# Graph attention turned round to 128 keys by 512 queries, with the expert stage split off

## The reference

```python
lK, lV = ln(x) @ Wlk, ln(x) @ Wlv + blv            # keys, values
local = where(adj, (masked_x @ Wlq) @ lK.T / 16, -1e9)
top = max(local.max(1), global_score, es)
le, ge, ee = exp(local - top), exp(global_score - top), exp(es - top)
denom = le.sum(1) + ge + ee
res = le/denom @ lV + ge/denom * gV + ee/denom * eV
x1 = x + maximum(res, masked_x)
xf = ln(x1); n = ln(xf) * ln_g + ln_b
xa = n @ attn_w.T + attn_b + xf
h = gelu(xa[expert] @ fc1[e].T + b1[e]); y = h @ fc2[e].T + b2[e]
out = x1 + gelu(y @ next_w.T + next_b)
```

## Time and profile before

| | us |
|---|---|
| median of 3 runs | 1241.9 (1238.49 to 1241.97) |
| span of the profiled execution | 1237.6 |
| PE / PE weight load busy | 1173.4 / 1003.3 |
| DVE / ACT / POOL busy | 782.8 / 550.7 / 458.5 |
| instructions | 21869 |

### The profile page before, as it was taken

The page is one execution under the profiler, slowest core; times in us unless marked ns, Lnnn a source line. Parts: engine busy times, 40 slices in busy tenths (PEclk is TensorE's granted clock), DMA queues, the critical chain, the costliest instruction groups (busy, mean ns, idle before and its releaser), DMA issues.

```text
span 1237.6 us, 21869 instructions
## 1 busy us (share of the span) xinstructions
PE 1173.4 (95%) x6524; PEld 1003.3 (81%) x6524; DVE 782.8 (63%) x1750; ACT 550.7 (44%) x981; POOL 458.5 (37%) x512
## 2 busy tenths in 40 slices
PE   4679999999999999999999999999988999999997
PEld 3557888888888888888888888888877887888886
DVE  6985555655556555565555555555577777877773
ACT  4534433344333443333433334433445565565654
POOL 4552223222232222322222322223237466655661
PEclk9799999999999999999999999999999999999999
DMA  7551111101111111111111111111346354454511
GB/s 231 176 148 33 56 34 34 47 34 55 34 34 46 34 55 34 34 42 38 48 42 34 42 38 43 46 34 42 99 163 195 99 177 151 163 195 131 174 69 51
DMA packets 70476, 100.15 MB, mean 81 GB/s; under 512 B 5936, under 2 KB 45872, under 8 KB 70448
## 3 DMA queue, kind: packets, MB, share of 16 engines
q1 hardware_dynamic: 70448, 99.81, 25.3%
HBM read 74.56 MB, written 16.84 MB: 74 GB/s over the span
## 4 chain that ended last, share of the span: by engine, by line
PE 76%; DVE 10%; issue 4%; ACT 2%; POOL 1%; DVEq 0%; ACTq 0%; POOLq 0%
PE u_ps L1269 19%; PE u_ps L1270 10%; PE s_ps L42 10%; PE s_ps L40 10%; PE s_ps L41 9%; PE pt_ps L1284 9%; DVE cst L953 2%; DVE xf L966 1%; DVE xn L966 1%; DVE h_lo L978 1%; DVE x_next L948 1%; DVE resm L943 1%; PE h_ps L40 1%; PE y_ps L40 1%; PE y_ps L42 1%
## 5 line engine op out<-in xcount | busy, mean ns | idle before, releaser
L1269 PE MATMUL u_ps<-v_sp,p_hi 128*128 128x512 f32 x1024 | 370.5, 397 | 2.6 <-DVE p_lo L878 2.6
L1121 ACT ACTIVATE p_hi<-pt_ps 128x512 fp32r<-128x512 f32 x256 | 153.2, 598 | 425.1 <-PE pt_ps L1284 425.1
L878 DVE TENSOR_TENSOR p_lo<-pt_ps,p_hi 128x512 fp32r<-128x512 f32 x256 | 176.9, 691 | 247.3 <-ACT p_hi L1121 245.6
L1270 PE MATMUL u_ps<-v_sp,p_lo 128*128 128x256 f32 x1024 | 287.7, 281 | 0.0
L783 POOL TENSOR_SCALAR bias<-adj 128x1024 f32<-128x1024 uint8 x126 | 132.9, 1055 | 405.3 <-DVE tops L885 391.3
L1269 PEld LDWEIGHTS u_ps<-v_sp,p_hi 128*128 128x128 f32 x1024 | 192.4, 188 | 48.9 <-DVE p_lo L878 3.5
L40 PE MATMUL s_ps<-lnT_hi,q_hi 128*128 128x512 f32 x512 | 221.7, 433 | 1.1 <-PEq L197 1.1
L885 DVE CUSTOM_DVE_ANT_0 scores<-s_ps,bias 128x512 f32<-128x512 f32 x256 | 176.3, 689 | 56.2 <-PE s_ps L42 55.9
L42 PE MATMUL s_ps<-lnT_hi,q_lo 128*128 128x512 f32 x512 | 202.0, 395 | 0.0
L41 PE MATMUL s_ps<-lnT_lo,q_hi 128*128 128x512 f32 x512 | 201.2, 393 | 0.0
L1270 PEld LDWEIGHTS u_ps<-v_sp,p_lo 128*128 128x128 f32 x1024 | 193.2, 189 | 9.5
(11 more groups left out here) (178 smaller groups left out, 1822.8 us busy)
## 6 DMA issues: line engine op xcount, KB each, us to landing
adj<-in_adj SPq DMA_DIRECT2D x64, 256.0 KB, 2.8
raw<-in_wffn SPq DMA_DIRECT2D x32, 512.0 KB, 4.6
u_scratch<-u_out SPq DMA_DIRECT2D x32, 258.0 KB, 2.4
u<-u_scratch SPq DMA_DIRECT2D x16, 516.0 KB, 4.7
xg<-in_x SPq DMA_DIRECT2D x8, 512.0 KB, 4.8
mg_raw<-in_mxT SPq DMA_DIRECT2D x8, 512.0 KB, 3.9
q_scratch<-q_out SPq DMA_DIRECT2D x16, 256.0 KB, 4.0
q_in<-q_scratch SPq DMA_DIRECT2D x32, 128.0 KB, 2.4
```

What stands on the lines that cost most here:

```text
L878: nc.vector.tensor_tensor(p_lo[:, c % 2], pt_ps[c % 2][:, :], p_hi[:, c % 2].bitcast(fp32), ALU.subtract).then_inc(plo_ready, 1)
L1121: nc.scalar.activation(p_hi[:, c % 2], pt_ps[c % 2][:, :], ACT.Copy).then_inc(phi_ready, 1)
L1269: nc.tensor.matmul(u_ps[:, :], p_hi[:, c % 2, js], v_sp[:, c * TG + j, :], start=c + j == 0, stop=False)
L1270: last = nc.tensor.matmul(u_ps[:, 0:D], p_lo[:, c % 2, js], v_sp[:, c * TG + j, 0:D], start=False, stop=c * TG + j == NT - 1)
```

## The change

The attention works on blocks of 512 queries (one for each expert: 256 rows of each half) and tiles of 128 keys: 8 blocks x 32 tiles = 256 steps. The scores come out with keys on the partitions, so that the probabilities need no transposing before they weigh the values. Now the probabilities move (512 queries) and the values are stationary (128 x 128). The scores of a whole block are kept in an SBUF ring of 38 slots, because the maxima of a query are known only after its 32nd tile; the weighing of a tile follows its scores by `LAG` = 37 steps. So there are 293 steps: 37 with scores alone, 219 with both, 37 with weighing alone. They are unrolled, not looped.

- **PE**, a step: `score` (6 matmuls of 512 columns), `weigh` (4 with `p_hi`, 2 with `p_lo`, 512 columns each). At a block's end come four transposes of the maxima (`turn_tops`), two steps later four more (`spread_tops`), and four small products (`add_up`), each behind the weighing of its step.
- **DVE**, a step: `centre` (scores minus spread maxima, from PSUM), `mask` (scores plus bias), `keep` (running maximum over the tiles, held in PSUM as `kept_ps`). Once a block: `pick_top`, 4 x `extra_scores`, `shares`, `take_second`.
- **ACT**, a step: two exponentials of 512 columns, one written rounded (`p_hi`), one whole (`p_all`).
- **POOL**, a step: the bias of 512 columns and `p_lo` = `p_all` minus `p_hi`.
- **SP**: the split values are written to `v_scratch` while preparing (8 x 1 MB) and read back in pairs of key tiles (512 KB) for each block; the adjacency comes re-laid in 256 KB pieces, one for four steps.
- The row sums come out of column 0, which is set to 1 in `lnf`; lines that fold column 0 back (`wlv0_b`, `xbar_fixed`, `qw` minus its first column) are added to the preparing. `lnf` is therefore written in 255 columns a row.
- The splits of the four weights, done on DVE beside the first scores before, are done on POOL at the start of the attention, and stored to DRAM.
- The experts stand in a block of their own behind a barrier. Results, split weights and rows are loaded back there; the tokens of expert 0 are prepared by a body -1 of its own. `turn_results`, `high_result` and `low_result` are gone from the bodies; POOL gets `extra_values` (12 instructions a body), which was the rank-one part in the attention.

```diff
+LEAD = 5
+LAG = KT + LEAD
+SLOTS = 38
+AHEAD = 2
-                        last = nc.vector.tensor_scalar(lnf[:, pp, j], xg[:, pp, j], mv[:, pp, j, 0:1], rstd[:, pp, j:j + 1],
+                        last = nc.vector.tensor_scalar(lnf[:, pp, j, 1:D], xg[:, pp, j, 1:D], mv[:, pp, j, 0:1], rstd[:, pp, j:j + 1],
...
+                def low_weight(y):
+                    pool.wait_ge(phi_ready, y + 1)
+                    pool.wait_ge(pall_ready, y + 1)
+                    wait(pool, pv_done, y - 1)
+                    nc.gpsimd.tensor_tensor(out=p_lo[:, y % 2], in0=p_all[:, y % 2], in1=p_hi[:, y % 3].bitcast(fp32),
+                                            op=ALU.subtract).then_inc(plo_ready, 1)
...
+                def centre(y):
+                    n, k = divmod(y, KT)
+                    if k == 0:
+                        dve.wait_ge(spread_done, n + 1)
+                    dve.wait_ge(masked, y + 1)
+                    nc.vector.tensor_tensor(scores[:, y % SLOTS], scores[:, y % SLOTS], mb_ps[:, :], ALU.subtract).then_inc(centred, 1)
+                def mask(t):
+                    dve.wait_ge(score_done, t + 1)
+                    dve.wait_ge(bias_ready, t + 1)
...
+                    nc.vector.tensor_tensor(scores[:, t % SLOTS], s_ps[t % 3][:, :], bias[:, t % 2], ALU.add).then_inc(masked, 1)
...
+                    nc.vector.tensor_tensor(top_keys[:, :] if k == LASTS else kept_ps[:, :], kept_ps[:, :], scores[:, t % SLOTS],
+                                            ALU.max).then_inc(kept, 1)
...
+                def exponentials(y):
+                    act.wait_ge(centred, y + 1)
+                    wait(act, pv_done, y - 2)
+                    nc.scalar.activation(p_hi[:, y % 3], scores[:, y % SLOTS], ACT.Exp, scale=SCALE).then_inc(phi_ready, 1)
+                    wait(act, plo_ready, y - 1)
+                    nc.scalar.activation(p_all[:, y % 2], scores[:, y % SLOTS], ACT.Exp, scale=SCALE).then_inc(pall_ready, 1)
...
+                for t in range(STEPS):
+                    n, k = divmod(t, KT)
+                    if t < TILES:
+                        score(t)
+                    if t >= LAG:
+                        weigh(t - LAG)
+                    if n > 0 and k == 0 and n <= BLOCKS:
+                        turn_tops(n - 1)
+                    if n > 0 and k == 2 and n <= BLOCKS:
+                        spread_tops(n - 1)
+                    ended = ends_block(t)
+                    if ended is not None:
+                        add_up(ended)
+                add_up(BLOCKS - 1)
...
+                for tt in range(TG):      # extra_values, POOL, once a body
...
+                        for r, row in enumerate((gvc_b, bev_b)):
+                            nc.gpsimd.tensor_scalar(kt_part[:, r], row[:, :], coef4[:, 1 + r, tt:tt + 1], 0.0,
+                                                    ALU.mult, ALU.add).then_inc(ktpart_ready, 1)
+                        nc.gpsimd.tensor_tensor(out=kt[:, tt], in0=kt_part[:, 0], in1=kt_part[:, 1], op=ALU.add).then_inc(kt_ready, 1)
```

More of the change, by code:

```diff
@@ L72, in sb, with region, place @@
                 size *= n
[L73 to L78 removed]
+            return size
+        def region(start, end):
+            position = [start]
+            def place(name, shape, dt=fp32):
+                buffer = nc.alloc_sbuf_tensor_at(name, shape, dt, offset=position[0])
+                size = size_of(shape, dt)
+                position[0] += size + -size % 32
+                assert position[0] <= end, (name, position[0], end)
+                return buffer
+            return place
         def ps(stack, name, shape=(P, CH)):
@@ L448, in group @@
                         for k in range(KD):
-                            last = nc.tensor.matmul(attc_ps[:, 0:D], lnb_c[:, k], w_raw[:, WATT, k], start=k == 0, stop=k == KD - 1)
+                            last = nc.tensor.matmul(attc_ps[:, 0:D], lnb_c[:, k], w_all[:, WATT, k], start=k == 0, stop=k == KD - 1)
                         last.then_inc(attc_done, 1)
@@ L458, in _ @@
                 groups(pe, group)
+                pe.wait_ge(xbar_ready, 2)
+                pe.wait_ge(gw_ready, 1)
+                for k in range(KD):
+                    last = nc.tensor.matmul(gw_ps[:, 0:P], ones[:, :], xbar_c[:, k], start=k == 0, stop=k == KD - 1)
+                last.then_inc(xbar_added, 1)
                 pe.wait_ge(wg_loaded, 48)
-                pe.wait_ge(gw_ready, 1)
-                pe.wait_ge(xbar_ready, 2)
+                pe.wait_ge(xbar_fixed, 1)
                 for n, w in enumerate((wgv_in, wq_in[:, 0])):
@@ L484, in gnn_moe_kernel @@
-        rden = sb(b, "rden", [P, 1])
-        table_in = sb(b, "table_in", [P, 1])
-        u_part = sb(b, "u_part", [P, D])
-        u_out = sb(b, "u_out", [P, ROWU])
-        kt_b = sb(b, "kt_b", [P, 3, D])
-        attention_end = nc.sbuf_base
-        assert starts["xg"] == starts["held"] and starts["lnf"] == starts["xg"] + 2 * 2 * CH * 4
-        assert attention_end <= starts["q_out"]
+        pb = ExitStack()
+        s_ps = [ps(pb, f"s_ps{i}") for i in range(3)]
+        u_ps = [ps(pb, f"u_ps{k}") for k in range(KD)]
@@ L495, in gnn_moe_kernel @@
+        pb.close()
+        HR = 4
         xt_ps = ps(ctx, "xt_ps")
@@ L509, in gnn_moe_kernel @@
-        pt_done, phi_ready, plo_ready, pv_done, upart_ready, u_ready = (
-            sem(n) for n in ("pt_done", "phi_ready", "plo_ready", "pv_done", "upart_ready", "u_ready"))
-        kpart_ready, ksum_ready, kt_ready = sem("kpart_ready"), sem("ksum_ready"), sem("kt_ready")
-        def steps(eng, step):
-            step(-1, here=False)
-            step(0)
-            with eng.Fori(1, NT - 2) as t:
-                step(t)
-            step(NT - 2, after=False)
-            step(NT - 1, ahead=False, after=False)
@@ L623, in bodies @@
         def bodies(eng, body):
+            body(-1, here=False, past=False)
             body(0, past=False)
@@ L1097, in body @@
                     finish(e, here, ahead, past, beyond)
-                steps(dve, step)
                 bodies(dve, body)
```

1082 lines of the change are left out of this document (543 added, 539 removed).

## The result

The changed kernel takes 1187.05 us in the median (4 runs, 1186.05 to 1189.12), the kernel before 1241.93 us (4 runs). The ratio is 0.957, with a 95% interval of 0.9547 to 0.9595. The forecast was 1192, in a range of 1163 to 1232. The profiled execution has a span of 1184.2 us, 53.4 less than before.

What follows compares the result with a forecast made beforehand. PE alone was taken to set the attention's pace. Preparing 90.5, filling 64, middle 619, emptying 52, closing 10, preparing of expert 0 48 and bodies 304 sum to 1187.5; plus 4.3 gives 1192 us, range 1163 to 1232.

Steps and rivals of the forecast that it cites:

- The 4.3 us added for the median: Whole kernel: the median of the runs was put 4.3 us above the profiled span.
- Preparing: Stretch before the first score: ends at 90.5 us, with +5 for colliding transfers and +3 for column 0's repair.
- The rival of the freed `lnf`: In preparing: 255 columns escape POOL's hold-up, so preparing shortens by 14 us, total 1178; chance 10%.
- Filling: The 37 steps of scores alone at the attention's start: 64 us in all.
- The allowances for extras and for adjacency behind the weight stores: In filling: 5 us for four pairs of `extra_scores`, 3 for the third adjacency piece.
- Middle: The 219 steps with scores and weighing: 2.79 us each, 611 us, with block ends 619.
- the block ends: Transposes and one-column products ending each block in the attention: 7 blocks x 1.2 = 8 us.
- Emptying: The 37 steps of weighing alone at the attention's end: 52 us, PE-bound, though barely.
- Closing and preparing of expert 0: Between attention and expert bodies: 10 us behind the last step, then 48 us of loads and chain standing alone.
- Bodies: The eight expert bodies: 304 us, from 306.3, with -7 for transposes gone and +5 for stretched DVE operations.
- the +5 for DVE instructions that stretch beside GpSimd: In the expert bodies: DVE operations with two SBUF inputs stretch while POOL runs, +5 us.
- DVE as the bound: Rival in the attention's middle: DVE's step passes 3.02 us and the kernel gets slower, 1277 to 1358 us; chance 12%.

Runs made afterwards that it cites:

- The thin version: Against the changed kernel, GpSimd works out only 4 of 256 columns of the constant part from the second expert on; 1180.21 us.

## Why the prediction was right, and where its terms were off

The mechanism was right: PE bounds before and after, 256 steps lose 0.44 us or a little more each, and half of that comes back at the ends. The sum of the terms was 1187.5 against a span of 1184.2, but four of them were off, by -6, -12, +7 and +6 us, and cancelled: that the whole came within 0.4% is partly luck. The 4.3 us added for the median were about 2: this profiled execution took 1186.05 us for its span of 1184.2.

- **Preparing, 90.5 forecast.** The first score came at 91.8, where 93.1 would follow from the term and GpSimd's two low queries (2 x 1.30). The transfers do fill it: DMA share 0.83, 283 GB/s, where the earlier trace rows had 0.67 and 200. The rival of the freed `lnf` fell: 398/405/2466 ns in 255 columns, as good as the 399/408/2470 of the earlier trace rows. The rule of the Trainium skill (VectorE: DVE Perf Modes, Mode 2×_2P — use both read ports for one tensor), that an odd and equal size still takes both ports, agrees with that. What the collisions with GpSimd's low values cost is shown by the run without them: 14.2 us of DVE's time, of which little would have reached the end.
- **Filling, 64 forecast, 58 measured.** The first weighing came at 149.90, 58.1 us behind the first score; by the forecast it was due at 154.5. The step was 1.36 as in the earlier trace rows. The allowances for extras and for adjacency behind the weight stores were too high: DVE had 0.6 us of waits for the bias there.
- **Middle, 619 forecast, about 608 measured** (first weighing at 149.90, the last step with a score ends near 757). The term took the pitch of the earlier trace rows, 0.2325, from the old step; in the new one twelve matmuls run at 0.227, which the earlier trace rows already had (1.36 / 6). That is 219 x 0.07 = 15 us less. Why the old step's scores ran slower is open: between the rows that gave 0.2325 stand only matmuls of 512 columns. Against it the block ends cost more, 13 us instead of 8 (a whole one takes 2.17: 89.21 - 32 x 2.72): the four one-column products, which I put at 0.3 from the transposes' row, take about 1 us.

```profile
239.35 1.05 PE L878 MATMUL mt_ps<-ident,uT 1*128 1x1 f32 x8
240.33 0.50 PE L50 MATMUL s_ps<-q_hi,lnT_hi 128*128 128x512 f32 x1
```

  The four calls are eight rows here, the next matmul starts 0.98 us behind them, and the one after that 0.34 later instead of 0.227: 1.1 us, eight times, six of them in the middle.
- **Emptying, 52 forecast, 59 measured.** The undisturbed step is 1.36, 37 of them 50.3 us; the rest are two sets of one-column products, two of transposes, a wait of 1.9 us for values, three of 0.8 us or less for `p_lo` and 2.1 us of waits for DVE and ScalarE at the block ends. The term left all of them out by taking 37 steps alone. "PE-bound, though barely" was the warning; it should have had a price.
- **Closing and preparing of expert 0, 10 + 48 forecast, 9.0 + 48.3 measured.** The experiments show that 12 to 15 of these 57 are not needed (the middle piece falls from 96.2 to 84.2 and 80.9): they are the loads, a result that is waited for although another was stored long before, and the wait for the last stores.
- **Bodies, 304 forecast, 310.4 measured.** The term that was too small is the +5 for DVE instructions that stretch beside GpSimd: -7 + 5 were to take 2 us off, and 4.1 came on. The mechanism was named, the place not: GpSimd's added part, 8.6 us a body here and not 6.8, pushes four low weights onto the residual and reaches `y_lo` as well. Over the four bodies before, PE waited 7.1 us, over four after it 12.0; 1.1 of the difference is for `nT_lo`, 2.8 for `h_lo`, 0.9 for `y_lo`. The thin version gives back 6.8 us in seven bodies, and with it the bodies would have come to 303.6. That is still 4 us above 306.3 - 7. Some 1.6 of them are the first nine matmuls of expert 0, which run 0.43 apart behind the bare stretch (granted clock 0.83 from 870 to 880 us, 1.00 from 880 on); the rest is not traced.
- **DVE as the bound (12%).** It fell, and the run with `keep` taken twice shows by how much: a DVE step is about 2.3 us, where I had 2.4 and put the turning point at 3.02. All three operations ran at 0.68 to 0.70 beside a GpSimd that was busy 74% of the time; the fear that they would be like `h_lo` did not come true. Each has an operand in PSUM, and no run tried them without one.

## What to carry to other kernels

When the busiest engine is bare in the middle, take instructions off it and count those that stay at a pitch read from a stream like the new one; then price the ends, for a deeper pipeline moves work from under cover into them. An engine that nobody waits for is not free: before giving it work, look at what its later instructions will run beside, and what is queued behind those. Loads for the next part belong under the previous part's bound steps, dealt out at the rate of what is left of the queue, not in one piece at its end.

## What the runs showed of the hardware

- DVE wrote PSUM at nearly the price of reading it: `kept_ps<-kept_ps,scores`, input and output in one PSUM tile, takes 699 ns for 512 columns, against 687 for `scores<-s_ps,bias`. With two such instructions and two that only read PSUM a round took 2.66 us, beside GpSimd.
- A matmul of one column by one is not cheap: four calls hold PE for 0.98 us, as long as four matmuls of 512 columns in this kernel (4 x 0.227 = 0.91).
- On GpSimd a product of 256 columns by a scalar takes 0.48 us, and one of 4 columns still 0.26 (median 268 and 275 ns); the addition falls from 0.74 to 0.20. Less work in as many instructions saves half to three quarters.
- Two DVE instructions with both inputs in SBUF took 1198 and 1135 ns in the mean where GpSimd's subtractions ran beside them, and 693 and 692 ns without. In three runs that took GpSimd's work away from one place, the collision was gone there; in one of them it came back at `y_lo`, 2.58 us for a pair instead of 1.54.
